# A routed feed-forward layer on one core: expert results added straight into the output by indirect transfers instead of through a table of results

## What is computed

```python
x = x + jnp.tanh(g_xattn[0]) * xattn(_layernorm(x), ctx_1024, ctx_1024, Wq, Wk, Wv, Wo)
x = x + jnp.tanh(g_ffn[0])   * ffn(_layernorm(x), router_w, w1, b1, w2, b2)

# ffn, per token row:
router_probs = jax.nn.softmax(x_flat @ router_w.T)
top_k_probs, top_k_idx = jax.lax.top_k(router_probs, 2)
top_k_probs = top_k_probs / (top_k_probs.sum(axis=-1, keepdims=True) + 1e-08)
cw = (one_hot(top_k_idx, E) * top_k_probs[..., None]).sum(axis=1)
for e in range(E):
    h = new_gelu(x_flat @ w1[e].T + b1[e])
    output = output + cw[:, e:e + 1] * (h @ w2[e].T + b2[e])
```

## Time and profile before

| | |
|---|---|
| median of three runs | 1292.09 us |
| the profiled execution | 1290.77 us |
| its span, first to last instruction | 1289.0 us |
| TensorE busy | 1244.2 us (97%) |
| VectorE busy | 1116.9 us (87%) |
| ScalarE busy | 1084.3 us (84%) |
| GpSimd busy | 553.5 us (43%) |
| chain that ended last | TensorE 82%, SP's queue 6%, GpSimd 4%, VectorE 3%, transfers 2% |
| moved by DMA | 112.93 MB, mean 88 GB/s |

### The profile page before, as it was taken

How to read it: one execution, slowest core, us unless ns; L and a number is a source line. 1 busy time by engine, 2 the same in 40 slices (tenths; PEclk the granted TensorE clock), 3 DMA queues, 4 the chain that set the end, 5 groups by cost and what they waited for, 6 DMA issues and landing times.

```text
span 1289.0 us, 42176 instructions
## 1 busy us (share of the span) xinstructions
PE 1244.2 (97%) x16259; PEld 623.0 (48%) x16259; DVE 1116.9 (87%) x1980; ACT 1084.3 (84%) x2196; POOL 553.5 (43%) x1213
## 2 busy tenths in 40 slices
PE   7999999999999999999999999999999999999992
PEld 2344444444444444444444444444444444499992
DVE  8899999999999999999999999999999999356434
ACT  2788998999898989899999999999999898866661
POOL 6324344353536262726252635445353512146542
PEclk9999999999999999999999999999999999999996
DMA  3332222212121212121212121222211110288886
GB/s 95 91 92 65 67 78 60 69 55 75 48 79 47 80 48 80 45 87 38 80 44 71 54 71 59 66 65 62 68 56 42 51 43 6 96 257 245 262 270 239
DMA packets 61092, 112.93 MB, mean 88 GB/s; under 512 B 13053, under 2 KB 36477, under 8 KB 60749
## 3 DMA queue, kind: packets, MB, share of 16 engines
q1 hardware_dynamic: 54187, 97.98, 25.9%
q0 software_dynamic: 4320, 8.99, 2.0%
q10 hardware_dynamic: 2385, 3.27, 0.7%
HBM read 52.77 MB, written 13.71 MB: 52 GB/s over the span
## 4 chain that ended last, share of the span: by engine, by line
PE 82%; SPq 6%; POOL 4%; DVE 3%; issue 2%; DMA 2%; ACT 0%; POOLq 0%; DVEq 0%
PE pv L911 31%; PE st L820 17%; PE mxp L874 13%; PE st L797 7%; PE st L1130 5%; PE mxp L1140 5%; SPq L415 4%; DVE mx L1679 2%; POOL kf L658 1%; PE mxp L881 1%; POOL ksp L663 1%; PE st L941 1%; POOL rows L722 1%; PE mxp L847 1%; DVE x_sb L1872 1%
## 5 line engine op out<-in xcount | busy, mean ns | idle before, releaser
L1679 DVE TENSOR_REDUCE mx<-mxp 128x2 f32<-128x1024 f32 x768 | 916.9, 1218 | 43.2 <-PE mxp L874 35.9
L1169 ACT ACTIVATE arena<-st 128x512 f32<-128x512 f32 (+1 forms) x1664 | 883.6, 597 | 64.4 <-PE st L820 50.1
L911 PE MATMUL pv<-arena 128*32 128x256 f32 x6656 | 531.6, 391 | 0.6 <-ACT pv_sb L1176 0.3
L820 PE MATMUL st<-qpack,kpack 51*128 51x256 bf16 (+1 forms) x3328 | 486.9, 272 | 3.0 <-DMA qpack<-mxT 2.6
L874 PE MATMUL mxp<-kpack,qpack 48*128 48x512 bf16 x1502 | 406.1, 383 | 1.5 <-DVE mx L1679 1.5
L820 PEld LDWEIGHTS st<-qpack,kpack 51*128 51x128 bf16 (+1 forms) x3328 | 192.4, 95 | 279.2 <-ACT arena L1169 153.1
L911 PEld LDWEIGHTS pv<-arena 128*32 128x32 f32 x6656 | 131.2, 108 | 173.8 <-issue 104.1
L689 POOL CAST mxs<-nmx 128x8 bf16<-128x8 f32 x64 | 12.2, 191 | 345.1 <-DVE nmx L1689 345.0
L874 PEld LDWEIGHTS mxp<-kpack,qpack 48*128 48x128 bf16 x1502 | 121.1, 93 | 68.5 <-issue 34.1
L1332 ACT ACTIVATE arena<-st,bias 128x256 f32<-128x256 f32 (+1 forms) x172 | 74.9, 437 | 46.2 <-PE st L1130 42.0
L732 POOL DMA_INDIRECT results<-ysb,idx x71 | 68.2, 961 | 79.9 <-DVE ysb L1814 54.2
(11 more groups left out here) (202 smaller groups left out, 983.7 us busy)
## 6 DMA issues: line engine op xcount, KB each, us to landing
kpack<-ksp SPq DMA_DIRECT2D x756, 50.0 KB
arena<-in_w12T SPq DMA_DIRECT2D x43, 576.0 KB
arena<-in_ctxT SPq DMA_DIRECT2D x15, 800.5 KB, 4.7
qpack<-qsp SPq DMA_DIRECT2D x187, 32.0 KB
xblk<-rows SPq DMA_DIRECT2D x28, 132.0 KB, 4.0
rows<-in_pads SPq DMA_DIRECT2D x8, 264.0 KB
arena<-results SPq DMA_DIRECT2D x8, 256.0 KB, 7.0
arena<-results ACTq DMA_DIRECT2D x8, 256.0 KB, 7.1
```

The lines of the kernel that those rows point to most:

```text
L820: ins = eng.matmul(ring[i][0:n, jj * N:(jj + 1) * N], kpack[rows, b % 2, g * JJ + jj, kt * P:kt * P + n], qpack[rows, b % 2, g * JJ + jj, ...
L911: ins = eng.matmul(pv[32 * j:32 * j + 32, 0:N], vaug[0:n, b % 2, kt, at:at + 32], pt[0:n, (2 * u + rg) % PT_BUFS, jj * N:(jj + 1) * N], st ...
L1169: eng.activation(pt[0:n, c % PT_BUFS, :], ring[bank_of["S", u, p]][0:n, :], ACT.Exp, scale=SCALE).then_inc(s_exp, 1)
L1679: eng.tensor_reduce(mx[:, tj, w, :], src[:, :, 0:WIN], AX.X, ALU.max).then_inc(s_red, 1)
```

## The change

- The table `results`, its read-back (`load_results`), the 16 adds and the eight output writes at the end are gone.
- `out` gets 512 spare rows (`DUMP`) behind its 4096; padding rows of a block go there, so the host cuts the output.
- SP writes `x_sb` of batch b to `out` (128 KB) at unit 36 of batch b+1 (`WRITE_AT`), for b = 0 to 14, and for the last batch behind the loads of block 10. It waits for `s_res` first. The spare rows are filled once with zeros.
- The token numbers that travel with the rows now name rows of `out`, so that both choices of a token go to one row.
- GpSimd's transfer of a tile adds to `out` (`compute_op=ALU.add`) in place of writing to `results`.
- Ahead of the first tile of every block but the first, GpSimd waits until all transfers of the block before have landed. Ahead of block 0 it waits for 16 of the 17 writes to `out`, ahead of position 31 for all 17.
- At the end SP waits for the landings of the indirect transfers, and nothing follows.

```diff
-                eng.dma_start(sums[k][:, tiles, :], back[:, tiles, :]).then_inc(s_sum[k][n], 16)
...
+            def write_rows(b):
+                eng.wait_ge(s_res, b + 1)
+                eng.dma_start(outs[:, b, :, :], x_sb[:, b * NT:(b + 1) * NT, :]).then_inc(s_out, 16)
...
+                    eng.dma_start(out[B * N:B * N + DUMP, :], pads[0:DUMP, 0:D]).then_inc(s_out, 16)
...
+                if b > 0 and r == WRITE_AT:
+                    write_rows(b - 1)
...
                 load_block(i)
+                if i == XS_BUFS + 2:
+                    write_rows(B - 1)
...
-            load_results(eng, 0)
-            for n in range(NPC):
-                eng.wait_ge(s_o, n + 1)
-                eng.dma_start(outs[:, n * PIECE // NT:(n + 1) * PIECE // NT, :, :],
-                              x_sb[:, n * PIECE:(n + 1) * PIECE, :]
-                              .rearrange("p (b t) d -> p b t d", t=NT)).then_inc(s_out, 16)
-            eng.wait_ge(s_out, 16 * NPC)
+            for i in range(YS_BUFS):
+                eng.wait_ge(s_ys[i], 16 * sum(tiles_of(j) for j in range(i, NBK, YS_BUFS)))
...
                 for j in range(tiles_of(i)):
                     eng.wait_ge(s_ysb, tiles_before(i) + j + 1)
+                    if j == 0 and i == 0:
+                        eng.wait_ge(s_out, 16 * B)
+                    if j == 0 and i == ORDER.index(FULL):
+                        eng.wait_ge(s_out, 16 * (B + 1))
+                    if j == 0 and i > 0:
+                        eng.wait_ge(s_ys[(i - 1) % YS_BUFS], writes(i - 1 + YS_BUFS))
                     if j > 0:
                         eng.wait_ge(s_hp, min(HC * (i + 3), CHUNKS))
                     eng.indirect_dma_start(
-                        results, bass.IndirectOffsetOnAxis(
+                        out, bass.IndirectOffsetOnAxis(
                             ap=idx[:, i % IDX_BUFS, j:j + 1].bitcast(U32), axis=0),
-                        ysb[:, i % YS_BUFS, j, :], None).then_inc(s_ys[i % YS_BUFS], 16)
+                        ysb[:, i % YS_BUFS, j, :], None, compute_op=ALU.add).then_inc(s_ys[i % YS_BUFS], 16)
...
-            for n in range(NPC):
-                own_x = x_sb[:, n * PIECE:(n + 1) * PIECE, :]
-                for k in range(2):
-                    eng.wait_ge(s_sum[k][n], 16)
-                    if k > 0:
-                        eng.wait_ge(s_dve, own)
-                    eng.tensor_tensor(own_x, own_x, sums[k][:, n * PIECE:(n + 1) * PIECE, :], ALU.add
-                                      ).then_inc(s_dve if k == 0 else s_o, 1)
```

More of the change, by code:

```diff
@@ L75 @@
 PADS = NE * 2 * SL + SPARE * SS
-Y_ROWS = 2 * B * N + PADS
+DUMP = 2 * SL
 CHUNKS = NBK * HC
@@ L81 @@
 XS_BUFS, W_BUFS, IDX_BUFS, YS_BUFS, BIAS_BUFS = 8, 4, 8, 4, 4
-PIECE = 4
-NPC = TILES // PIECE
 NX = NE + 1
@@ L86 @@
 SCATTERED = 16 * 2 * NT
+WRITE_AT = 36
 TABLES = [P, P, 2 * TILES, HC * NE, NX, NX, FULL, NX * NE]
@@ L333, in build @@
         ysb = sb("ysb", [P, YS_BUFS, SJ, D])
-        sums = [pt_f[:, 0:TILES * D].rearrange("p (t d) -> p t d", d=D),
-                vaug_f[:, 0:TILES * D].rearrange("p (t d) -> p t d", d=D)]
-        results = nc.dram_tensor("results", (Y_ROWS, D), F32, kind="Internal").ap()
         rows = nc.dram_tensor("rows", (NE * CAP + SPARE * SS, ROW), F32, kind="Internal").ap()
@@ L394, in build @@
         s_ys = [sem(f"s_ys{i}") for i in range(YS_BUFS)]
-        s_sum = [[sem(f"s_sum{k}{i}") for i in range(NPC)] for k in range(2)]
-        s_o, s_out = sem("s_o"), sem("s_out")
+        s_out = sem("s_out")
         block = ctx.enter_context(nc.Block())
[L401 to L405, removed]
-            for n in range(NPC):
-                tiles = slice(n * PIECE, (n + 1) * PIECE)
-                eng.dma_start(sums[k][:, tiles, :], back[:, tiles, :]).then_inc(s_sum[k][n], 16)
         xs = x.rearrange("(b p t) d -> p b t d", p=P, t=NT)
+        outs = out[0:B * N, :].rearrange("(b p t) d -> p b t d", p=P, t=NT)
         def pack_key_rows(eng, b, g, part, rg):
@@ L588, in _ @@
                                   pads[ex * 2 * SL:(ex + 1) * 2 * SL, :]).then_inc(s_pad, 16)
-            outs = out.rearrange("(b p t) d -> p b t d", p=P, t=NT)
-            load_results(eng, 0)
-            for n in range(NPC):
-                eng.wait_ge(s_o, n + 1)
-                eng.dma_start(outs[:, n * PIECE // NT:(n + 1) * PIECE // NT, :, :],
-                              x_sb[:, n * PIECE:(n + 1) * PIECE, :]
-                              .rearrange("p (b t) d -> p b t d", t=NT)).then_inc(s_out, 16)
-            eng.wait_ge(s_out, 16 * NPC)
+            for i in range(YS_BUFS):
+                eng.wait_ge(s_ys[i], 16 * sum(tiles_of(j) for j in range(i, NBK, YS_BUFS)))
         @block.gpsimd
@@ L1341, in _ @@
                     exp_logits(B - 1)
-            load_results(eng, 1)
         @block.vector
@@ L1864, in _ @@
                             plan_step(2, n - 20)
-            for n in range(NPC):
-                own_x = x_sb[:, n * PIECE:(n + 1) * PIECE, :]
-                for k in range(2):
-                    eng.wait_ge(s_sum[k][n], 16)
-                    if k > 0:
-                        eng.wait_ge(s_dve, own)
-                    eng.tensor_tensor(own_x, own_x, sums[k][:, n * PIECE:(n + 1) * PIECE, :], ALU.add
-                                      ).then_inc(s_dve if k == 0 else s_o, 1)
-                    if k == 0:
-                        own += 1
 _INS = ["x", "ctxT", "gates", "wq", "wk", "wv", "woT", "rwT", "w12T", "ident", "tables", "pads"]
@@ L1903, in _lay_out @@
             np.triu(np.ones((P, P)), 1), np.ones((P, P)),
-            (np.arange(P)[:, None, None] * TILES + np.arange(TILES)[:, None]
-             + np.arange(2) * B * N).reshape(P, 2 * TILES),
+            np.repeat((np.arange(B)[:, None] * N + np.arange(NT)[None, :]).reshape(1, TILES)
+                      + np.arange(P)[:, None] * NT, 2, axis=1),
             a["L0_ffn_b1"].reshape(NE, HC, P).transpose(2, 1, 0).reshape(P, HC * NE),
@@ L1910, in _lay_out @@
         ], 1).astype(np.float32),
-        "pads": np.concatenate([np.zeros((PADS, D + 1)), 2 * B * N + np.arange(PADS)[:, None],
+        "pads": np.concatenate([np.zeros((PADS, D + 1)), B * N + np.arange(PADS)[:, None] % DUMP,
                                 np.zeros((PADS, 2))], 1).astype(np.float32),
@@ L1927 @@
                                    kind="ExternalInput").ap())
-    out = nc.dram_tensor("out_x", (B * N, D), F32, kind="ExternalOutput").ap()
+    out = nc.dram_tensor("out_x", (B * N + DUMP, D), F32, kind="ExternalOutput").ap()
     build(nc, *args, out)
     r = _run(nc, [arrays], core_ids=[0])
-    return r.results[0]["out_x"].reshape(B, N, D)
+    return r.results[0]["out_x"][0:B * N].reshape(B, N, D)
```

## The result

The changed kernel takes 1400.74 us (median of five runs, 1398.54 to 1401.31) against 1292.19 us before. The ratio of the runs is 1.0816, with a 95% interval of 1.0792 to 1.0841; the two medians alone give 1.084. It is 8% slower; forecast were 1350 us in a range from 1300 to 1428. The profiled execution took 1401.31 us, 1.8 more than its span.

A forecast was written before the change was run, and what follows sets the result against it. TensorE, busy 138.9 of 142 us, was taken to pace the experts' stage, with a 19.5 us end behind. The new serial chain gave 1170.7 + 43 x 4.1 = 1347.0, with 3.1 outside the span 1350 us, range 1300 to 1428.

The forecast's parts named there:

- L: GpSimd, experts' stage: time from the start of an issue to its landing, forecast 4.1 us, bounds 2.23 to 5.9.
- The step of the second tile: GpSimd, two-tile blocks: second issue starts 1.26 us after the first, an issue taking 0.96; counted 27 times.
- From landing to next issue: GpSimd, between blocks: 0.05 us from a landing to the next issue, counted 42 times.
- The start: Experts' stage: chain starts with the second tile of block 0 at 1134.54, waiting for TensorE as before.
- The end: After the last expert's landing: read-back, 16 adds and output writes removed, the whole 19.5 us won.
- (a): Experts' stage: adding transfer is light and traffic doesn't hurt, so faster, 1273 us; chance 0.07.
- (b): Adding transfers: reading the destination is dear, L 6.5 or so, time 1453 us; chance 0.13.
- (c): TensorE, experts' stage: clock falls to 1.2 GHz in the pauses, its work doubles and bounds, 1408 us; chance 0.07.
- What was costed at nothing: SP's 17 writes, covered by its 234.1 us of waiting, and GpSimd's waits for them: 0 us.
- The four scatters of the last batch: GpSimd, behind blocks 9 to 12: issued in the shadow of a landing, cost 0, about 30 us later.
- What was said of the profile after: Experts' stage: GpSimd waits on landings, two-tile blocks 5.4 us apart, TensorE 65% busy, DMA 0.6, span ending within 1 us.

## Why the prediction was right, and where its sum was wrong

The mechanism was right, and the direction with it: one serial chain of 43 landings on GpSimd in place of a stage bound by TensorE. The formula was end = start + 27 steps + 42 pauses + 43 L. With what the chain and the timeline show, 1138.27 + 27 x 1.86 + 42 x 0.75 + 43 L reaches the last landing at 1396 if L is 4.1 on the mean. The forecast was 1347.0 for the end of the span, and 1399.5 was measured. Term by term:

- **L, 4.1 forecast, 4.1 measured, -0.3 us.** The agreement is luck, for it is made of other parts. The chain with plain writes (222.4 us from the second start to the last landing, less 27 x 1.26 and 42 x 0.75) has 3.65 on the mean, not 4.1; the scatters are delayed less than the loads of the earlier trace rows were. The addition brought some 0.4 more, its longer issue included. The prediction had a plain landing of 4.1 and let the addition and the thinner traffic cancel: two errors of opposite sign.
- **The step of the second tile, +16.2 us.** I took an adding issue to be as long as a plain one, 0.96 us. It is 1.55, so the step is 1.86. The prediction bounded L for an operation that no row shows and forgot to bound its issue.
- **From landing to next issue, +29.4 us.** This is the largest miss. I took 0.05 us, from VectorE's end to an issue in the earlier trace rows. But VectorE's row at 1264.36 is the second tile of the block; the issue at 1264.71 waits for the first, which was ready when the second was under way. In the trace the first ends at 1264.44, so 0.27 us lay between and not 0.02. I read the wrong tile. And from a landing it is longer still: the measured 0.75 us is the same with plain writes and with additions.
- **The start, +3.7 us.** The first transfer starts at 1133.24 and not at 1129.52. In that trace the first load of the experts is issued 1.0 us later (1118.36 against 1117.38), the first weights take 5.07 us to land, and TensorE's clock is at 0.66 between 1124 and 1129. The kernel that differs in the addition alone starts at 1130.67, so it isn't the writes that were added to SP's queue. Why it was late in this trace stays open.
- **The end, +3.5 us.** The removed 19.5 us were measured rightly, but not all of them are won, as the closing of the program was hidden under them.

3.7 + 16.2 + 29.4 - 0.3 + 3.5 = 52.5, and 1347.0 + 52.5 = 1399.5. That the time lies in the range is luck in part. The range was wide for L alone: its upper end stood for L = 5.9, 77 us above the forecast. L took none of that; terms that had no bounds, the pause and the step above all, used up 50.

**The rivals.** (a) gave 1273 and would have needed L = 2.3 with pauses of 0.05. Even a plain write alone on the DMA engines takes 2.24 + 0.75 = 2.99 a turn. By the fit of the Trainium skill, "DMA: Bandwidth & Descriptors", section "Anatomy of one DMA — SWDGE (gpsimd) path", a tile takes an estimated 2.15 us: the quiet plain write agrees with 2.24, the quiet adding one is at 3.2, and under load the two are at 3.65 and 4.1 on the mean, so the fixed cost held for plain and quiet alone. (b) had 6.5 for L: out, at 3.2 quiet. (c) was half right. The clock did fall in the pauses (0.83 on the mean from 1160 on, 1.00 from 1138 to 1160), but 0.83 is two thirds of the time at 2.4 GHz and one third at 1.2, and from 1160 on no more than 0.2% of the chain lies on line 1126: TensorE is off it. It was on the chain at the lower clock in other kernels with the chain of waits, for about 5% with eight buffers and 8% with small weight loads.

**What was costed at nothing** on SP held: its 17 writes are not on the chain of the changed kernel. The four scatters of the last batch behind blocks 9 to 12 lay in the shadow of landings, as said: the blocks 9 to 13 begin 6.1 to 6.6 us apart (1201.30 to 1226.45), like other two-tile blocks. They came 34 to 41 us later than before, not 30. TensorE waited 5.5 us for these rows, off the chain; with eight buffers the same wait was on it.

**What was said of the profile after:** GpSimd's waits on landings, yes; two-tile blocks 5.4 us apart, no, about 6 (1276.03 to 1282.00); TensorE busy 65% of the stage, was 61% (57% from 1160 on); DMA share 0.6, was 0.56 (0.52 from 1160 on); the span ends within 1 us of the last landing, no, 3.5.

## What to carry to other kernels

A transfer that costs nothing while nobody waits for it costs its whole landing as soon as the next one must wait for it. Before a table and its read-back are traded for additions in place, count the waits that order the additions and multiply by issue, landing and the pause between them: here 42 such waits cost 122 us to win some 14. If an order is needed, let several independent targets take turns, so that landings overlap, and take issue, pause and landing each from a row of its own, with bounds for each.

## What the runs showed of the hardware

- An indirect transfer of 128 rows of 512 bytes that adds to its destination occupies GpSimd for 1.55 us, one that writes 0.96. From its start it lands in 3.2 us with idle DMA engines, the plain one in 2.24.
- From the landing of a transfer to the start of the next one that waited for it on GpSimd, 0.74 to 0.77 us pass in nearly every turn, in the writing and in the adding kernel alike.
- A program whose last work is a GpSimd transfer ends 3.5 us after the landing of an adding one (1396.0 to 1399.5) and 5.2 after that of a plain one (1362.2 to 1367.4 in the changed kernel without the addition).
- The clock of TensorE fell in pauses that come every 5 to 6 us with TensorE busy 57% of the time, to 0.83 on the mean of the stretch. It fell to 0.50 by 1182.9, by 1196.6 and by 1213.6, and no pause of TensorE between 1170 and 1214 was longer than 2.5 us.
